# Neighbour sum of a point-cloud kernel: eight batches to a body of its loop, where a body held two

## The reference, cut to what matters

```python
x = _L0_xattn_ref(x, ctx_4096, ...)          # attention + x, normalised over T
x = _L1_xattn_ref(x, ctx_4096, ...)
# L2, for each of the 32 batches:
xk = x.transpose(0, 2, 1)[bidx, idx]          # idx: the 30 neighbours of a point
agg = jnp.einsum('bnkc,bnk->bnc', xk, att)    # att: their softmax weights
x = x + agg.transpose(0, 2, 1)
# L3
out = _chunk_attn(ctx_4096, ...) + x
return (out - mu) * jax.lax.rsqrt(var + EPS)  # mu, var over T
```

## Time and profile before

| | us |
|---|---|
| time, median of 3 runs | 6258.06 (6256.48 to 6260.03) |
| time of the profiled execution | 6258.18 |
| its span, first to last instruction | 6256.4 |
| PE busy | 5448.7 (87%) |
| DVE busy | 5585.7 (89%) |
| ACT busy | 4490.2 (72%) |
| POOL busy | 3506.1 (56%) |
| granted TensorE clock, mean | 0.938 of full |

### The profile page before, as it was taken

One profiled execution on the slowest core, in us unless ns is written; L12 is line 12 of the kernel. 1 busy time (PEld: TensorE's weight loads), 2 busy tenths in 40 slices (PEclk: granted clock), 3 DMA queues, 4 the chain that ended last, 5 costly groups with the idle time before them and its releaser, 6 DMA issues. The chain is left out here.

```text
span 6256.4 us, 228198 instructions
## 1 busy us (share of the span) xinstructions
PE 5448.7 (87%) x82804; PEld 3392.0 (54%) x82804; DVE 5585.7 (89%) x7936; ACT 4490.2 (72%) x17146; POOL 3506.1 (56%) x3600
## 2 busy tenths in 40 slices
PE   7888888888888888888888888888859769999999
PEld 3455555555555555555555555555533357777776
DVE  7999999999999999999999999999945787777776
ACT  7888888888888888888888888888845623333333
POOL 4466666666666666666666666666670033333332
PEclk9999999999999999999999999999969889999999
DMA  2333333333333333333333333333323023333332
GB/s 46 95 94 110 90 99 98 94 97 95 95 107 98 96 108 91 100 98 93 97 92 99 107 98 94 110 90 100 88 101 75 0 72 96 85 88 85 89 93 72
DMA packets 656108, 568.86 MB, mean 91 GB/s; under 512 B 557824, under 2 KB 579584, under 8 KB 620960
## 3 DMA queue, kind: packets, MB, share of 16 engines
q1 hardware_dynamic: 618016, 284.53, 19.4%
q10 hardware_dynamic: 36864, 268.45, 12.1%
HBM read 384.78 MB, written 67.24 MB: 72 GB/s over the span
## 5 line engine op out<-in xcount | busy, mean ns | idle before, releaser
L769 ACT ACTIVATE prob<-SC,row_max 128x64 f32<-128x64 f32 x6144 | 1836.1, 335 | 376.6 <-DVE row_max L1123 368.0
L886 POOL TENSOR_TENSOR prob<-prob,row_rec 128x512 f32<-128x512 f32 x768 | 800.6, 1042 | 1379.4 <-DVE row_rec L1131 1369.3
L769 ACT ACTIVATION_READ_ACCUMULATOR prob<-SC,row_max 128x1 f32 x6144 | 1387.0, 228 | 0.0
L1115 DVE FIND_INDEX8 nbr<-top,dist 128x8 uint16<-128x1024 f32 x1024 | 1234.5, 1217 | 0.0
L1108 DVE MAX8 top<-dist 128x8 f32<-128x1024 f32 x1024 | 1190.4, 1203 | 1.5
L1110 DVE MATCH_REPLACE8 dist<-top,dist 128x1024 f32<-128x1024 f32 x768 | 923.6, 1207 | 0.0
L627 PE MATMUL SC<-k_bd,q_t 128*64 128x256 f32 x6144 | 877.4, 409 | 0.0
L1801 ACT ACTIVATE dense<-DM 128x512 f32<-128x512 f32 x512 | 305.4, 596 | 750.1 <-PE DM L1760 750.0
L1909 DVE TENSOR_TENSOR d_oh_a<-lo,iota_a 128x4096 bf16<-128x4096 bf16 x256 | 583.8, 2290 | 241.2 <-PE DM L1760 240.3
L648 PEld LDWEIGHTS PT<-ident,prob 128*128 128x128 f32 x3072 | 358.0, 144 | 791.9 <-issue 770.4
L589 PEld LDWEIGHTS G<-table,low_all 128*128 128x128 bf16 x24576 | 664.8, 96 | 169.1 <-issue 92.5
(11 more groups left out here) (216 smaller groups left out, 9463.1 us busy)
## 6 DMA issues: line engine op xcount, KB each, us to landing
low_all<-low_scratch ACTq DMA_DIRECT2D x256, 1024.0 KB, 4.8
k_bd<-k_t SPq DMA_DIRECT2D x3072, 16.0 KB, 1.9
placed<-compact SPq DMA_DIRECT2D x256, 192.0 KB, 3.9
ctx<-in_ctx SPq DMA_DIRECT2D x32, 512.0 KB, 3.3
mask<-in_mask SPq DMA_DIRECT2D x32, 512.0 KB, 8.8
xb<-in_x SPq DMA_DIRECT2D x32, 512.0 KB, 3.4
x_scratch<-xb SPq DMA_DIRECT2D x32, 512.0 KB, 4.0
y_scratch<-y_b SPq DMA_DIRECT2D x32, 512.0 KB, 6.7
```

Of the source, the lines that this page charges most:

```text
L769: last = act.activation(prob[:, s % 4, g * CHUNK:(g + 1) * CHUNK], SC[:, s % 2, g * CHUNK:(g + 1) * CHUNK], ACT.Exp, bias=row_max[:, s % 2 ...
L886: pool.tensor_tensor(pr, pr, row_rec[:, r % 2, :].unsqueeze(2).to_broadcast([128, 8, CHUNK]), ALU.mult).then_inc(normed, 1)
L1115: last = dve.max_index(nbr[:, uu % BPB, t, k * 8:(k + 1) * 8], best, row)
```

## The change

A body holds eight batches: BPD = 8, BODY_D = 4. The first eight batches and the last eight are written out, and the loop runs twice over eight. The buffers and their semaphores stay at two, under a name of their own (BUFD = 2), and are indexed by u % BUFD. A body uses each slot TURNS_D = 4 times, so a wait for a transfer counts i x TURNS_D + u // BUFD + 1. The load of `nb` two batches ahead is left out in the last two batches, as before.

```diff
-BPD = 2
+BPD = 8
+BUFD = 2
+TURNS_D = BPD // BUFD
 BODY_D = N // BPD
...
-        nb = sb("nb", [128, BPD, NT * KP], U16)
+        nb = sb("nb", [128, BUFD, NT * KP], U16)
...
-        x2_in = [sem(f"x2_in{u}") for u in range(BPD)]
+        x2_in = [sem(f"x2_in{u}") for u in range(BUFD)]
...
-                if not (isinstance(i, int) and i == BODY_D - 1):
+                if not (isinstance(i, int) and i * BPD + u + BUFD >= N):
                     sp.wait_ge(dstep, START + b(D_STEPS, D_STEPS))
                     sp.sem_inc(passed, 1)
-                    sp.dma_start(nb[:, u, :], dram["nbr"][b(1, BPD)]).then_inc(nb_in[u], 16)
+                    sp.dma_start(nb[:, u % BUFD, :], dram["nbr"][b(1, BUFD)]).then_inc(nb_in[u % BUFD], 16)
...
-                pe.wait_ge(x2_in[u], START + (i + 1) * 16)
+                pe.wait_ge(x2_in[u % BUFD], START + (i * TURNS_D + u // BUFD + 1) * 16)
...
-                dve.wait_ge(out_done[u % BPD], START + j * 16)
-                read_sum(b, u % BPD, 0)
+                dve.wait_ge(out_done[u % BUFD], START + (i * TURNS_D + u // BUFD) * 16)
+                read_sum(b, u, 0)
```

More of the change, by code:

```diff
@@ L1603, in neighbour_sum @@
         placed = sb("placed", [128, 2, 4, 3, QG, 8], BF16)
[L1604 to L1607, removed]
+        x2 = sb("d_x2", [128, BUFD, T])
+        y3 = sb("d_y3", [128, BUFD, T])
+        x2_t = sb("x2_t", [128, BUFD, NT, 128])
+        y = sb("d_y", [128, BUFD, T])
         dense = [sb(f"dense{c}", [128, 8, HALF]) for c in range(2)]
@@ L1617, in neighbour_sum @@
         consts_in = sem("d_consts_in")
-        x2_in = [sem(f"x2_in{u}") for u in range(BPD)]
-        y3_in = [sem(f"y3_in{u}") for u in range(BPD)]
+        x2_in = [sem(f"x2_in{u}") for u in range(BUFD)]
+        y3_in = [sem(f"y3_in{u}") for u in range(BUFD)]
         copied_in = sem("copied_in")
-        nb_in = [sem(f"nb_in{u}") for u in range(BPD)]
+        nb_in = [sem(f"nb_in{u}") for u in range(BUFD)]
         split = sem("d_split")
@@ L1640, in neighbour_sum @@
         normed = sem("d_normed")
-        out_done = [sem(f"out_done{u}") for u in range(BPD)]
+        out_done = [sem(f"out_done{u}") for u in range(BUFD)]
         dstep = sem("d_dstep")
@@ L1673, in _ @@
                 sp.dma_start(dst, dram[name]).then_inc(consts_in, 16)
-            for u in range(BPD):
+            for u in range(BUFD):
                 sp.wait_ge(out_done[u], START)
@@ L1695, in body @@
                 b = counter(i, u)
-                if not (isinstance(i, int) and i == BODY_D - 1):
+                if not (isinstance(i, int) and i * BPD + u + BUFD >= N):
                     sp.wait_ge(dstep, START + b(D_STEPS, D_STEPS))
                     sp.sem_inc(passed, 1)
-                    sp.dma_start(nb[:, u, :], dram["nbr"][b(1, BPD)]).then_inc(nb_in[u], 16)
+                    sp.dma_start(nb[:, u % BUFD, :], dram["nbr"][b(1, BUFD)]).then_inc(nb_in[u % BUFD], 16)
                 spread_blocks(i, u, 1)
                 if not is_first(i, u):
-                    before, slot = counter(i, u - 1), (u - 1) % BPD
+                    before, slot = counter(i, u - 1), (u - 1) % BUFD
                     if not is_last(i, u):
@@ L1721, in _ @@
             sp.wait_ge(normed, START + N)
-            sp.dma_start(dram["out"][N - 1], y[:, BPD - 1, :]).then_inc(out_done[BPD - 1], 16)
-            for u in range(BPD):
-                sp.wait_ge(out_done[u], START + BODY_D * 16)
+            sp.dma_start(dram["out"][N - 1], y[:, (BPD - 1) % BUFD, :]).then_inc(out_done[(BPD - 1) % BUFD], 16)
+            for u in range(BUFD):
+                sp.wait_ge(out_done[u], START + N // BUFD * 16)
         @block.tensor
@@ L1737, in weighted_sum @@
                 for m in range(4 * part, 4 * part + 4):
-                    last = pe.matmul(AG[:, hh, :], x2_t[:, u, m, :], dense[hh][:, m, :], start=(m == 0), stop=(m == 7))
+                    last = pe.matmul(AG[:, hh, :], x2_t[:, u % BUFD, m, :], dense[hh][:, m, :], start=(m == 0), stop=(m == 7))
                 if part == 1:
@@ L1764, in body @@
                         before = counter(i, u - 1)
-                        weighted_sum(before, (u - 1) % BPD, 1, t)
+                        weighted_sum(before, u - 1, 1, t)
                     if t in (4, 5):
@@ L1856, in body @@
                 b = counter(i, u)
-                pool.wait_ge(x2_in[u], START + (i + 1) * 16)
-                pool.wait_ge(y3_in[u], START + (i + 1) * 16)
+                pool.wait_ge(x2_in[u % BUFD], START + (i * TURNS_D + u // BUFD + 1) * 16)
+                pool.wait_ge(y3_in[u % BUFD], START + (i * TURNS_D + u // BUFD + 1) * 16)
                 pool.sem_inc(passed, 1)
-                pool.tensor_tensor(y3[:, u, :], y3[:, u, :], x2[:, u, :], ALU.add).then_inc(xy_ready, 1)
+                pool.tensor_tensor(y3[:, u % BUFD, :], y3[:, u % BUFD, :], x2[:, u % BUFD, :], ALU.add).then_inc(xy_ready, 1)
                 if not is_last(i, u):
-                    split_weights(counter(i, u + 1), (u + 1) % BPD, not is_first(i, u))
+                    split_weights(counter(i, u + 1), u + 1, not is_first(i, u))
                 if not is_first(i, u):
@@ L1874, in _, with indices @@
             dve.wait_ge(consts_in, START + 16 * len(CONSTS))
-            def indices(b, u, j):
+            def indices(b, i, u):
                 n = 0
```

32 lines of the change are left out of this document (16 added, 16 removed).

## The result

| | before | after |
|---|---|---|
| time, median of 4 runs each, us | 6259.05 (6256.48 to 6262.41) | 6214.15 (6212.12 to 6219.41) |
| ratio, 95% interval | | 0.9929 [0.9912, 0.9946] |
| span of the profiled execution, us | 6256.4 | 6212.5 |

The kernel is faster, as forecast, by 43.9 us of span where 53.6 were predicted. 6214 lies 10 us above the predicted 6204 and 1 us above the range's end.

The account below looks back on a forecast made before the run. The prediction took PE to bound the neighbour sum, its idle time mostly at 13 taken jumps. Span 6256.4 - 53.6 = 6202.8, plus 1.8 beyond the span, gave 6204.6, stated as 6204 us; range 6194 to 6213.

Parts of the forecast that it names:

- step 1: Jumps of the neighbour-sum loop: one taken where there were 13, 12 x 4.47 = 53.6 us less.
- step 2: Loop entry and exit, one each as before: PE's 1.04 us stall at 5124 moves and costs the same, 0.
- The period: Neighbour-sum batches without a jump: 70.46 us a pair, from PE's 34.69 a batch plus a DVE, SP, PE wait.
- steps 3 and 4: Neighbour-sum buffers and transfers keep size and place, and wait counts from registers or constants cost alike: 0 each.
- step 5: Instruction fetches in the neighbour sum: SP's or POOL's remaining jump between 0 and 2.6 us, taken as 0.
- last sign of being wrong: In the next profile's neighbour sum: new stalls of PE inside a batch without a branch would refute the forecast.
- The page's rule: Sequential prefetch, stall at far branches: small engines' remaining jump dearer, at most 2.6 us each; sum unmoved.
- Rival B: Neighbour sum: the DVE, SP, PE loop tightens, copies land 0.5 us later in 28 batches, 14 us, 6218; chance 0.10.
- Rival D: Neighbour sum: small engines' fetches stall SP ahead of its first-half copies, 78 us at 2.6 a batch, 6282; chance 0.03.
- E: Neighbour sum: the stalls are loads of x2, not jumps, so nothing changes, 6258; chance 0.02.

Follow-up runs that it names:

- e13: The changed kernel with the four weighted sums of a batch behind tiles 0, 2, 4 and 6, not 0, 1, 4 and 5: 6177.37 us.
- e14: The kernel before the change (two batches to a body) with the weighted sums behind tiles 0, 2, 4 and 6: 6232.81 us.
- e5: The kernel before the change with 64 more transpositions in batch 0, moving the code behind by 128 instructions: 6298.18 us.
- e1: The changed kernel with four batches to a body in place of eight, five taken jumps: 6259.51 us.
- e11: All 32 batches written out, no loop, with the weighted sums behind tiles 0, 2, 4 and 6, not 0, 1, 4 and 5: 6172.73 us.
- e4: The changed kernel with the load of x2 issued later in the batch: 6221.63 us.
- e6 to e8: All 32 batches written out, with the result stored later (6203.0 us), the second half's copies held back (6205.77), or both (6204.94).
- e10: All 32 batches written out, with x2, y3 and result transfers cut to 8 columns and `placed` copies to 24; other values than the reference: 6186.88 us.
- e15: e14 with 64 more transpositions in batch 0, moving the code behind by 128 instructions: 6252.58 us.
- e16: e11 with 64 more transpositions in batch 0, moving the code behind by 128 instructions: 6170.50 us.
- e9: The kernel with four batches to a body (e1) with 32 more transpositions in batch 0, moving the code behind by 64 instructions: 6246.73 us.

## Why the prediction was off, by its own steps

- *What bounds the kernel, and the jumps (step 1)*: right. One taken jump of L1655 is left. The 4.47 us came back as 4.62 where nothing else disturbed the comparison (e13, e14). But it was called "the price of a jump", and it is the price at one placement: 39 / 13 = 3.0 more with the code moved by 128 instructions (e5); with four batches to a body (e1), the stops at borders that this placement brought ate eight jumps' gain.
- *Entry and exit (step 2)*: the 1.04 us at 5124 isn't the loop's entry. It stands at 5124.15 now too (1.16), in the middle of straight code. It was the one long stop at a block's border in that trace, and I explained it away.
- *The period (the section before the steps)*: it held. From batch 2 to 31, without the three distances above, a batch takes 35.28 us on the mean, where 35.23 was used. But PE's "own work" of 34.69 a batch held waits of its own: with the sums apart a batch takes 34.30 (e11).
- *Buffers and waits (steps 3 and 4)*: nothing in the trace speaks against 0.
- *Code that is fetched (step 5)*: the step that failed. I costed it at 0, since no stop of PE "is for code" behind the last jump. Three batches were too few, and the place was lucky. The prediction's own last sign of being wrong, new stalls of PE inside a batch without a branch, is what came. In the changed kernel such stops are 11.0 us of idle time in twelve pieces where 1.3 were, and the three distances that hold the longest of them make up 9.5 of the 10.8 us missing between batch 2 and batch 31.
- *The page's rule*: the prediction noted that the sum would move if a crossing of a 16 KiB block were not "mostly hidden" (the Trainium skill, Runtime: NRT & Kernel Launch, Instruction fetch mechanics), and gave that no chance of its own. That is what happened on PE: stops of up to 1.9 us in straight code. On the four small engines the prediction had the remaining jump dearer by that page, up to 2.6 us. By its own figure of 512 instructions that did not follow: a body of eight batches is 262 on SP, 314 on ACT, 376 on DVE and 222 on POOL, counted in the trace. Their branches of L1655 lasted 40 to 74 ns, and 0 was right for them.
- *Rival B* had a time near the result (6218) by another mechanism, copies that land later. The waits for DVE and `placed` are 10.0 us, or 11.4 with the one of batch 7, under the 15 forecast without B, so B isn't it. Rival D didn't appear, as SP's branch lasts 45 to 55 ns. E fell with the 12 waits that are gone.
- *The range*: its upper end rested on half of B. A bound for step 5 from the 1.04 us at 5124, once a batch at the worst, would have reached well past 6213.

Open: why delaying single transfers (e4, e6 to e8) gains so little when taking nearly all their bytes away (e10) removes the stops; the copies of `placed` for the first half, next to the dense run, weren't moved. And why a refill at a jump takes 3.4 us at one placement and 4.1 at another (e14, e15) was not tried.

## What to carry to other kernels

When a stream of short instructions is unrolled, look for stops that lie a multiple of one number of instructions apart (256 here), whatever name the view gives the wait, and shift the code by half a block before trusting the price of a jump read from one kernel; the number may be the placement's. Where fetches can't keep up, spread the long instructions among the short ones: that order was worth 35 us here (some 16 of them, by the estimate above, not for code), against 44 for the change itself, and together with straight code 86 of 6259. A stall that a trace shows only once still needs its cause before it is costed at nothing.

## What the runs showed of the hardware

- PE's blocks are not always there in time. At 80 instructions a microsecond (96 DM matmuls and their loads in 2.4 us), with the DMA engines busy for a third of the time, a border costs up to 1.9 us; with them busy for 0.04 of it, one border cost 0.6 and no other as much as 0.15 (e10).
- 64 extra transpositions at the head of a stage, free in one kernel (e16), made another 39 us slower (e5), by what they did to the placement of a loop's target.
- The view can give a stop at a block's border to another engine: 6.9 us "for ACT" in e1 lie at block borders.
- A stop of 1.6 us can be followed by a stretch partly at 1.2 GHz (a granted 0.74 on the mean of 6.5 us): 8 AG matmuls took 5.37 us in place of 3.68.
- A jump whose target stands one matmul before the end of its block waits for two blocks in turn, 3.66 + 3.66 us (e9).
